# Eight of 16 softmax heads get their maximum subtracted by TensorE in PSUM, v's high part is copied by ScalarE, the negated means go, and the orders are laid out anew

## The reference

```python
mod = (_silu(L0_c) @ L0_wmod).reshape(L0_c.shape[0], 6, 1, -1)
h = _layernorm(x, axis=-1) * (1 + ca) + sa
...
q = (x @ Wq + bq).reshape(b, h, dh, t)
k = (x @ Wk + bk).reshape(b, h, dh, t)
v = (x @ Wv + bv).reshape(b, h, dh, t)
attn = jnp.einsum('bhdt,bhds->bhts', k, v) * temperature
attn = jax.nn.softmax(attn, axis=-1)
out = jnp.einsum('bhdt,bhts->bhds', q, attn)
...
x = x + ga * _L0_attn_ref(h, L0_attn_Wq, L0_attn_bq, L0_attn_Wk, L0_attn_bk, L0_attn_Wv, L0_attn_bv, L0_attn_temperature)
h = _layernorm(x, axis=-1) * (1 + cb) + sb
x = x + gb * _L0_ffn_ref(h, L0_ffn_w_gate, L0_ffn_w_up, L0_ffn_w_down)
```

## Time and profile before

| | us |
|---|---|
| median of 3 runs | 612.01 (610.42 to 612.53) |
| span of the profiled execution (it has no other time beside it) | 611.3 |
| TensorE busy | 558.3 |
| VectorE busy | 568.7 |
| ScalarE busy | 555.9 |
| GpSimd busy | 507.3 |

### The profile page before, as it was taken

One profiled execution on the slowest core, in us unless ns is written; L12 is line 12 of the kernel. 1 busy time (PEld: TensorE's weight loads), 2 busy tenths in 40 slices (PEclk: granted clock), 3 DMA queues, 4 the chain that ended last, 5 costly groups with the idle time before them and its releaser, 6 DMA issues.

```text
span 611.3 us, 15522 instructions
## 1 busy us (share of the span) xinstructions
PE 558.3 (91%) x4336; PEld 385.6 (63%) x4336; DVE 568.7 (93%) x1124; ACT 555.9 (91%) x2281; POOL 507.3 (83%) x710
## 2 busy tenths in 40 slices
PE   4588999999999999999999999999999999998874
PEld 2465556666666666666666666666666666666653
DVE  5568799999999999999999999999999999999986
ACT  2499899999999999999999999999999999999621
POOL 5544478999999999999999999999999999988741
PEclk9669899999999999999999999999999999999878
DMA  5655556546655556555655556655655556652000
GB/s 156 179 142 143 129 152 163 145 133 170 170 140 147 149 155 173 159 157 137 172 144 143 149 155 171 171 145 139 170 144 141 152 153 174 164 143 58 10 10 26
DMA packets 87888, 86.12 MB, mean 141 GB/s; under 512 B 8566, under 2 KB 83548, under 8 KB 87804
## 3 DMA queue, kind: packets, MB, share of 16 engines
q1 hardware_dynamic: 85372, 83.10, 50.4%
q10 hardware_dynamic: 2432, 2.03, 1.2%
HBM read 47.29 MB, written 37.81 MB: 139 GB/s over the span
## 4 chain that ended last, share of the span: by engine, by line
ACT 52%; PE 18%; issue 13%; DVE 12%; POOL 3%; ACTq 1%; DVEq 0%; POOLq 0%
ACT probs L825 47%; DVE neg_max L1005 6%; PE score_ps L1502 6%; PE bank L1581 5%; PE bank L1570 3%; ACT hT L835 2%; DVE silu_g L1123 2%; ACT hid_T L859 2%; PE bank L1548 2%; PE bank L1606 1%; ACT q_T L841 1%; DVE h_mag L975 1%; POOL hid_q L367 1%; PE bank L1520 1%; DVE h_mag L979 1%
## 5 line engine op out<-in xcount | busy, mean ns | idle before, releaser
L825 ACT ACTIVATE probs<-score_ps,neg_max 128x256 f32<-128x256 f32 x1024 | 483.5, 552 | 5.4 <-DVE neg_max L1005 4.3
L1005 DVE TENSOR_REDUCE neg_max<-score_ps 128x4 f32<-128x1024 f32 x256 | 312.1, 1219 | 19.5 <-PE score_ps L1502 16.8
L825 ACT ACTIVATION_READ_ACCUMULATOR probs<-score_ps,neg_max 128x1 f32 x1024 | 292.4, 286 | 0.0
L1502 PE MATMUL score_ps<-v_stack,k_stack 128*128 128x256 f32 x1024 | 234.9, 333 | 24.2 <-ACT probs L825 21.7
L1502 PEld LDWEIGHTS score_ps<-v_stack,k_stack 128*128 128x128 f32 x1024 | 156.0, 194 | 108.2 <-ACT probs L825 85.1
L1548 PE MATMUL bank<-probs,q_z 128*32 128x256 f32 x2048 | 132.6, 389 | 0.0
L1548 PEld LDWEIGHTS bank<-probs,q_z 128*32 128x32 f32 x2048 | 57.6, 111 | 42.4 <-issue 3.2
L1606 PEld LDWEIGHTS bank<-wd_T,hid_T 118*128 118x128 f32 x384 | 52.7, 201 | 7.6 <-ACT hid_T L859 1.3
L1606 PE MATMUL bank<-wd_T,hid_T 118*128 118x128 f32 x384 | 56.0, 286 | 0.5 <-ACT hid_T L859 0.5
L1570 PE MATMUL bank<-wgu_T,h_T 128*128 128x352 f32 x128 | 52.0, 488 | 1.7 <-ACT h_T L848 0.5
L367 POOL TENSOR_TENSOR hid_q<-hid_r,hid_sc 128x704 f32<-128x704 bf16 x31 | 43.0, 1387 | 7.6 <-DVE hid_r L362 7.5
(11 more groups left out here) (119 smaller groups left out, 880.9 us busy)
## 6 DMA issues: line engine op xcount, KB each, us to landing
split_dram<-kv_hi SPq DMA_DIRECT2D x124, 128.0 KB, 2.6
split_dram<-kv_lo SPq DMA_DIRECT2D x124, 128.0 KB, 2.6
k_stack<-split_dram SPq DMA_DIRECT2D x124, 128.0 KB, 4.5
v_stack<-split_dram SPq DMA_DIRECT2D x31, 512.0 KB, 4.2
mod_bc<-mod_dram SPq DMA_DIRECT2D x32, 256.0 KB, 4.0
x_in<-in_L_attn_x_dram SPq DMA_DIRECT2D x32, 128.0 KB, 3.1
out_dram<-out_t SPq DMA_DIRECT2D x32, 128.0 KB, 3.6
split_dram<-kv_hi ACTq DMA_DIRECT2D x4, 128.0 KB, 2.4
```

Of the source, the lines that this page charges most:

```text
L825: nc.scalar.activation(probs[p][:, h, a, :], score_ps[:, j % 4, a, :], ACT.Exp, bias=neg_max[:, p, n:n + 1], accum_out=row_sum[:, p, h, a: ...
L1005: nc.vector.tensor_reduce(neg_max[:, p, 4 * u:4 * u + 4], score_ps[:, lo:lo + 2, :, :].rearrange("p b a n -> p (b a) n"), AX.X, ALU.max, n ...
L1502: done = nc.tensor.matmul(score_ps[:, j % 4, a, :], k_stack[p][:, h, 128 * a:128 * a + 128], v_stack[p][:, h // R, :], start=True, stop=True)
```

## The change

- Of the 16 heads of a batch the eight with an odd number (`SHIFTED`) no longer have their negated maximum as a bias of the exponential. A new task `shift` on TensorE adds it to the scores in PSUM: one matmul of an identity with the maxima of the head's two halves, each repeated over 256 columns, 512 columns in all. The exponential of such a head waits for `shifted` and not for `maxed`. `neg_max` becomes F32R for it, and VectorE makes a copy of the identity once.
- The second score matmul of a head no longer starts an accumulation group of its own.
- v's high part is copied out of PSUM by ScalarE (`v_hi` in the scalar stream). k's high part waits for it.
- The negated means nm1 and nm2 are gone; the two normalisations subtract the mean straight from the statistics.
- TensorE waits for fewer semaphores before it writes a shared bank (`wait_bank`).
- All five orders are new, with lags that are one or two steps shorter; TAIL is 36 instead of 39, and the tasks of the last batches are listed anew.

```diff
-TAIL = 39
+TAIL = 36
+
+SHIFTED = (1, 3, 5, 7, 9, 11, 13, 15)
...
-        neg_max = sb("neg_max", [128, 2, H * 2])
+        neg_max = sb("neg_max", [128, 2, H * 2], F32R)
+        ident_r = sb("ident_r", [128, 128], F32R)
...
+        def mean_of(stats, c, a):
+
+            return stats[:, c % 2, 1 + 3 * a:2 + 3 * a]
...
             for a in range(2):
-                ve.tensor_scalar(h2_c[:, a, :], x1[:, c, a, :],
-                                        nm2[:, a:a + 1], rstd2[:, a:a + 1],
-                                        ALU.add, ALU.mult).then_inc(h2_c_made, 1)
+                ve.tensor_scalar(h2_c[:, a, :], x1[:, c, a, :], mean_of(stats2, c, a), rstd2[:, a:a + 1],
+                                 ALU.subtract, ALU.mult).then_inc(h2_c_made, 1)
...
             def exps(b, c, j):
                 p, h = c % 2, head(j)
-                if j % 2 == 0:
+                if j in SHIFTED:
+                    act.wait_ge(shifted, b * len(SHIFTED) + SHIFTED.index(j) + 1)
+                else:
                     act.wait_ge(maxed, b * (H // 2) + j // 2 + 1)
...
+                    if j in SHIFTED:
+                        nc.scalar.activation(probs[p][:, h, a, :], score_ps[:, j % 4, a, :], ACT.Exp,
+                                             accum_out=row_sum[:, p, h, a:a + 1]).then_inc(exped, 1)
+                    else:
...
+            def v_hi(b, c):
+                wait_batches(act, kv_ps_made, b + 1)
+                wait_dma(act, split_stored, b - 2, STORES * 16)
+                nc.scalar.activation(halves(kv_hi[c % 2][:, 1, :]), kv_rows(1), ACT.Copy).then_inc(v_hi_made, 1)
...
                 at(k, 7, exps, 10)
                 at(k, 7, exps, 11)
+                at(k, 5, v_hi)
+                at(k, 11, hidT_out, 1)
...
-            def minus_mean(nm, stats, p):
-                return nc.vector.tensor_reduce(nm[:, :], stats[:, p, 1:6:3].unsqueeze(2), AX.X, ALU.max, negate=True)
...
             def k_hi(b, c):
-                wait_batches(dve, kv_ps_made, b + 1)
+                dve.wait_ge(v_hi_made, b + 1)
...
                     done = nc.tensor.matmul(score_ps[:, j % 4, a, :], k_stack[p][:, h, 128 * a:128 * a + 128],
-                                            v_stack[p][:, h // R, :], start=True, stop=True)
+                                            v_stack[p][:, h // R, :], start=(a == 0), stop=True,
+                                            skip_group_check=True)
                 done.then_inc(scored, 1)
 
+            def shift(b, c, j):
+                if j not in SHIFTED:
+                    return
+                if b == 0 and j == min(SHIFTED):
+                    pe.wait_ge(ident_r_made, 1)
+                pe.wait_ge(maxed, b * (H // 2) + j // 2 + 1)
+                nc.tensor.matmul(score_ps[:, j % 4, :, :], ident_r[:, :],
+                                 neg_max[:, c % 2, 2 * j:2 * j + 2].unsqueeze(2).to_broadcast([128, 2, T]),
+                                 start=False, stop=True, skip_group_check=True).then_inc(shifted, 1)
```

More of the change, by code:

```diff
@@ L1419, in _ @@
             last(gate2, 29)
+            last(residual2, 29)
             last(silu, 31, 0)
@@ new lines, in step @@
+                at(k, 8, mix, 0)
+                at(k, 7, scores, 5)
+                at(k, 7, shift, 3)
+                at(k, 8, mix, 1)
+                at(k, 8, mix, 2)
+                if k == 2:
+                    condition()
+                at(k, 8, mix, 3)
+                at(k, 7, scores, 6)
+                at(k, 7, scores, 7)
+                at(k, 7, shift, 5)
+                at(k, 8, mix, 4)
+                at(k, 10, up_proj, 1)
+                at(k, 7, scores, 8)
+                at(k, 7, scores, 9)
@@ new lines, in step @@
+                at(k, 7, shift, 7)
+                at(k, 8, mix, 5)
+                at(k, 8, mix, 6)
+                at(k, 7, scores, 10)
+                at(k, 8, mix, 7)
+                at(k, 7, shift, 9)
+                at(k, 7, scores, 11)
+                if k == 6:
+                    gates()
+                at(k, 5, x_transpose)
+                if k == 10:
+                    ff_transpose(2)
+                at(k, 11, hid_transpose, 0)
+                at(k, 11, hid_transpose, 1)
@@ new lines, in _ @@
+            last(scores, 29, 0)
+            last(shift, 28, 15)
+            last(scores, 29, 1)
+            last(down_proj, 24, 1)
+            last(gate_proj, 26, 0)
+            last(up_proj, 26, 0)
+            last(scores, 29, 2)
+            last(scores, 29, 3)
+            last(shift, 29, 1)
+            last(gate_proj, 26, 1)
+            last(scores, 29, 4)
+            last(mix, 28, 0)
+            last(scores, 29, 5)
+            last(shift, 29, 3)
+            last(mix, 28, 1)
+            last(mix, 28, 2)
@@ new lines, in _ @@
+            last(scores, 29, 6)
+            last(mix, 28, 3)
+            last(scores, 29, 7)
+            last(shift, 29, 5)
+            last(up_proj, 26, 1)
+            last(scores, 29, 8)
+            last(mix, 28, 4)
+            last(scores, 29, 9)
+            last(shift, 29, 7)
+            last(mix, 28, 5)
+            last(mix, 28, 6)
+            last(mix, 28, 7)
+            last(scores, 29, 10)
+            last(scores, 29, 11)
+            last(shift, 29, 9)
+            last(hid_transpose, 25, 1)
@@ new lines, in _ @@
+            last(hid_transpose, 25, 0)
+            last(x_transpose, 31)
+            last(scores, 29, 12)
+            last(scores, 29, 13)
+            last(shift, 29, 11)
+            last(down_proj, 25, 0)
+            last(down_proj, 25, 1)
+            last(h2_transpose, 27)
+            last(q_proj, 31)
+            last(scores, 29, 14)
+            last(scores, 29, 15)
+            last(shift, 29, 13)
+            last(kv_proj, 31)
+            last(scores, 30, 0)
+            last(scores, 30, 1)
@@ new lines, in _ @@
+            last(shift, 29, 15)
+            last(gate_proj, 27, 0)
+            last(scores, 30, 2)
+            last(gate_proj, 27, 1)
+            last(scores, 30, 3)
+            last(shift, 30, 1)
+            last(up_proj, 27, 1)
+            last(scores, 30, 4)
+            last(up_proj, 27, 0)
+            last(mix, 29, 0)
+            last(scores, 30, 5)
+            last(mix, 29, 1)
+            last(shift, 30, 3)
+            last(mix, 29, 2)
+            last(mix, 29, 3)
+            last(scores, 30, 6)
@@ new lines, in _ @@
+            last(mix, 29, 4)
+            last(scores, 30, 7)
+            last(mix, 29, 5)
+            last(shift, 30, 5)
+            last(mix, 29, 6)
+            last(mix, 29, 7)
+            last(scores, 30, 8)
+            last(shift, 30, 7)
+            last(scores, 30, 9)
+            last(hid_transpose, 26, 1)
+            last(scores, 30, 10)
+            last(hid_transpose, 26, 0)
+            last(scores, 30, 11)
+            last(shift, 30, 9)
+            last(down_proj, 26, 0)
+            last(h2_transpose, 28)
```

782 lines of the change are left out of this document (434 added, 348 removed).

## The result

The changed kernel takes 648.6 us (median of 4 runs, 648.1 to 649.5) where the kernel before takes 612.3 (610.4 to 612.9). The ratio is 1.0606, with a 95% interval of 1.0576 to 1.0637. The forecast was 592.0, with a range of 583 to 603.

The account below looks back on a forecast made before the run. VectorE was to become the bound at 16.48 us per batch, 16.55 with waits, 0.63 less than before; 31 x 0.63 = 19.5 us off the 611.3 us span gives 591.8, a median of 592, range 583 to 603.

Parts of the forecast that it names:

- with the same two instructions, no dearer: GpSimd's normalisations: subtracting the mean straight from the statistics costs nothing more, so GpSimd's work stays 15.95 us per batch.
- TensorE thus needs about 14.5 of the 17.18 us: TensorE's 16.6 us per batch less 2.7 of weight-load waits; with the shifts added it comes to 16.4 to 17.2.
- TensorE becomes the bound: Rival: at 0.30 us a shift TensorE needs 16.9 us per batch, 603 us, between 597 and 609; chance 0.16.
- the shift holds the scores up: Rival: TensorE's queue between shift and next scores; at 0.44 us a shift need 18.0, time 637 us; chance 0.05.
- A shift at 0.24 to 0.34 us: TensorE's added 512-column matmuls, 8 per batch: 1.9 to 2.7 us per batch, the lower end taken.
- The sum over one engine at a time: Work per batch: ScalarE 15.92, GpSimd 15.95, VectorE 16.48 us; VectorE bounds, and with waits the period is 16.55.
- 0.093 us for a bias: ScalarE's exponentials without a bias, 16 per batch, each save 0.093 us: 1.49 us per batch.
- v's copy, and k_hi's wait for it at nothing: v's high part: ScalarE gains 0.26 us per batch, VectorE loses 0.33; VectorE's wait before k's high part costs nothing.
- my 1.6 without cover: VectorE's wait for ScalarE's copy of v: up to one pair of exponentials, 1.6 us, if no maximum covers it.
- with the same other instructions there in the new order: VectorE's tightest stretch of the score-bank loop: 3.69 us of work against a 3.73 us loop, leaving 0.04 us of waiting.
- rstd1's wait, start and end: GpSimd's 0.6 us per batch wait before rstd1 goes; start unchanged within 2 us, end (34.0 us) within 1.5.

Follow-up runs that it names:

- the base: The changed kernel with negated means in two buffers, added by GpSimd in place of the subtraction: 637.5 us, ratio 1.0397 to the kernel before.
- the move that shortens it: GpSimd's hid_r subtraction put behind normalise1 and h2_add: 638.9 us against 637.5 with shifts and added negated means, 618.8 against 625.1 in the new orders alone.

## Why the prediction was wrong, by its steps

- **"with the same two instructions, no dearer".** This step failed and decided the result. Subtract in place of add costs 0.35 us each, 1.4 us per batch. GpSimd, which I had at 15.95 us under a bound of 16.48, came to set 18.28: 17.0 busy, and 1.28 idle that I had counted as room. The edit alone costs the old kernel 36 us. The slip went through the rivals too: none has GpSimd as the bound.
- **"TensorE thus needs about 14.5 of the 17.18 us", and 16.4 to 17.2 with the shifts.** This failed too. With GpSimd cured the kernel is still 4% slower, and the chain, 64% of it on TensorE, sets 17.99 us in the new orders, and 17.45 in the old. I took the waits of its weight loads for room. Taking 8 x 0.22 us from the 17.45 of the old orders leaves 15.7 at most, 1.2 more than my 14.5, and I did not price the cuts of mix, 0.35 us each. The rival "TensorE becomes the bound" was nearest to the mechanism, with a price of 603 us, where 637.5 was measured. The rival "the shift holds the scores up" had 18.0 us and 637, which the base hits; that is luck, as it needed 0.44 us a shift, and a shift in a run took 0.22. By the busy share of weight loads (the Trainium skill, "Trainium Kernel Development and Optimization", "Performance Expectations") TensorE would have room still, 69% in the base. The matmul share, 99%, is nearer to what the chain shows here, but it was 97% already where ScalarE led, so neither share settles it.
- **A shift at 0.24 to 0.34 us.** Nearly right: 0.22 in a run, just under the lower bound. The Trainium skill, "TensorE: Matmul & The Clock Gate", section "Back-to-back issue gap", has 216 ns for 512 columns as the gap of an isolated matmul, which agrees, and 131 ns for a sustained stream, which no run here shows. But a shift stands also between a maximum and its exponentials, 0.48 us where it waits.
- **The sum over one engine at a time.** With 4 shifts ScalarE should have had 16.4 us by my price of a bias, and TensorE, at 15.7 + 0.9, 16.6. The period was 17.26, with the chain half on TensorE (51%) and a third on ScalarE (33%). My reading, which no run isolates, is that four engines above 90% pass work around in a ring, and the ring is longer than each one's work.
- **0.093 us for a bias.** Right for one exponential: 0.27 against 0.36 from its start to its read. Over a batch ScalarE's busy time fell from 17.15 to 16.58 us only, not to 15.92. Busy time counts the whole of the last instruction ahead of each wait, and ScalarE now waits more often; how much of the difference that is stays open. It was worth nothing, as ScalarE was no longer what bound.
- **v's copy, and k_hi's wait for it at nothing.** In the new orders that held. In the old ones, with the copy badly placed, it costs 95 us or 3.1 per batch, the fall of the clock included, twice my 1.6 without cover.
- **"with the same other instructions there in the new order".** I compared what stands in the orders, not what runs beside it on GpSimd. VectorE's exponent rose from 0.28 to 1.09 us, which is most of what lies between my 16.48 for VectorE and the 17.38 measured. With shifts the move that shortens it gains nothing; without them it gains 9 us.
- **rstd1's wait, start and end.** rstd1's wait is gone from the list, and both ends moved by under 2 us, as forecast.

The steps don't add up to one sum, since each takes effect only where its engine sets the pace: the subtraction costs the old kernel 5.7%, and taking it out of the changed one gives back 2.1 points. In the changed kernel, with the subtraction out, the parts of the other 4.0% are read from ratios of runs: the new orders 2.3 points, the shifts in them 2.7 more, v's copy on ScalarE 1.1 back. What stays open is the last 5 us of the new orders (1.0085): a batch in the middle takes 17.23 against 17.18 us there, which makes 1.5 us, so most of the 5 lies outside the middle. Open too is why the shifts cost 1.4% in the old orders and 2.7% in the new (1.0507 against 1.0233). The cuts of mix and the VectorE instructions held by GpSimd are candidates, and no run decides between them.

## What to carry to other kernels

Before you call two instructions of GpSimd equally dear, look for both operations in a trace: the operation counts, not only the shape. When you give work to an engine, take its room from the distance between its instructions along the chain, with every change between kinds of matmul in it, and not from the waits of its weight loads, nor from idle time as such: GpSimd kept 1.07 of its 1.23 us idle when it became the bound. And when an order changes, look at which instructions of VectorE and GpSimd now run at the same time.

## What the runs showed of the hardware

- GpSimd, tensor_scalar with two operands per partition on 128x128 fp32: add then multiply 0.45 us (0.53 for one of the two in the old orders), subtract then multiply 0.80 to 0.88, whether the operand lies in a tile of its own or in the statistics.
- TensorE: after a piece of matmuls with 32 columns of weights the next full ones take 0.20 us longer, and each such piece has 0.15 us of its own beside 0.43 per 8 matmuls.
- VectorE's int16 tensor_scalar on 128x256: 0.28 us alone, up to 1.09 beside a GpSimd instruction of 1.53 us. The wait is seen only in the length of VectorE's instruction, not as idle time, and the instruction ends 0.15 us behind GpSimd's.
